# A Perceiver layer in fp32: attention chains per tile of 128 tokens instead of per half, small V weights, 64-row score products, swapped K columns

## The chip, the cores and the metric

One core of one Trainium2 chip. The metric is device time in microseconds (us) of one execution; the profile comes from one profiled execution of the same program.

## The reference, cut to what matters

Three layers run one after the other on 8 batches of 64 tokens (512 tokens) of 256 numbers, with a context of 8 batches of 1601 rows.

```python
x = x + xattn(layernorm(x), ctx)      # scores without a softmax: (Q K^T) V = Q (K^T V), then wo, residual, layer norm
x = x + attn(layernorm(x))            # causal over 64 tokens, 16 heads of 16, softmax
x = x + ffn(layernorm(x))             # attention with rotary q and k (k and v through a rank of 64), softmax, rms norm,
                                      # then a gated shared MLP and 8 experts W2 weighted by the top 2, rms norm
```

The rotary step of the third layer is `stack([x1*cos - x2*sin, x1*sin + x2*cos])` over neighbouring pairs of a head's 16 numbers. The attention of a batch is `softmax(q k^T / 4) v` for each of 16 heads.

## The kernel before, in words

The 512 tokens are four tiles of 128 tokens (two batches each). The kernel calls two tiles a half. Everything is in SBUF; there are eight PSUM banks.

*Context.* For each of the 8 batches the context (1601 x 256) is loaded in three chunks, each split into a rounded high part (ScalarE, step `split`, L514) and a low part (VectorE, L1051), and TensorE forms the Gram matrix of the batch (`gram`, banks 0 and 1, `gram_tile`). From the Gram matrix come, in the steps `evac`, `cross1` to `cross4`, the products with the key and value weights (banks 6 and 7); with the fourth batch of a half, `cross2_product` also multiplies the column sums by the value weights (`scol`).

*Chains.* For each half there is a chain: `xo_product` and `xo` (output projection and layer norm of the cross attention), `norm1`, `turn_z` (transpose), `proj1` (q, k, v of 256 tokens at a time), then for each tile `score_product` (L787: four matmuls of 128 rows by 256 columns; the keys stand in `kblk`, where the 32 rows of each pair of heads fill only their own quarter of the columns), `score` (VectorE: causal bias, maximum, subtraction; ScalarE: exponential, L550), `turn_p` (eight transposes, copied to `probT`), `sums` (sum and reciprocal), `values` (L809: eight matmuls with `probT` as the weights of 128 columns and `vblk` as 64 moving columns), the division by the sums into `on` (L1149), `turn_o` (four transposes and two VectorE operations into `aT`, L1159 and L1160) and `project` (output projection). Then `norm2`, `turn_z`, `proj2` (q; the shared rank of k and v in `kvcT`; k and v from the lower and upper 64 rows of it; q and k each multiplied by a rotation matrix `rot`, VectorE combining with sine and cosine), the same attention steps again, `rms1` and `turn_x`. The chains use PSUM banks 2 to 5, all four by `proj1` and `proj2`, and two each by the tiles.

*Dense part.* For a half: 16 `hidden_product`s in all are 8 per half (12 matmuls of 256 columns each), two `shared_product`s, eight `experts_product`s (12 matmuls of 512 columns), in banks 0, 1, 6, 7; ScalarE applies Silu (L611), VectorE multiplies, ScalarE and GpSimd split the result. Experts are summed into `Z` on VectorE (L1229), `finish` scales and adds (rstd by a power on GpSimd, L408), SP stores each tile.

*Order.* All engines walk one list of steps in the same order (`steps_in_order`: opening, first half, second half, closing); each engine runs its share of every step, in order, with semaphore waits between the engines. So a step that waits holds back whatever stands behind it on its engine. In the opening list 16 of 24 Gram chunks are done before the first half's chain; that chain lies between the other eight; the second half's chain lies between the dense steps of the first half; the closing list is the dense part of the second half. In the closing list `finish` of tiles 0, 1 and 2 stand between expert steps, and only `finish` 3 stands behind the last.

An fp32 matmul shows in the trace as two records, a transpose and a matmul on the split (fp32r) parts as one.

## Time and profile before

| what | value |
|---|---|
| median of 3 runs | 270.0 us (269.54 to 271.69) |
| the profiled execution's own time | 269.51 us |
| its span, first to last instruction | 267.7 us |
| mean granted TensorE clock | 0.992 of full |
| TensorE matmul busy | 243.5 us, 91% |
| VectorE busy | 177.8 us, 66% |
| ScalarE busy | 119.2 us, 45% |
| GpSimd busy | 69.4 us, 26% |

The time of an execution is that between its begin and end; the span lies inside it and is 1.8 us shorter here. A row of the trace names engine, line, operation, result and operands, shapes, count, then busy time. Matmuls overlap each other in the pipeline, so the distance from the start of one group to the start of the next, divided by the records between, tells what a record costs a busy TensorE; the durations shown are longer.

### The profile page before, as it was taken

The page shows a single profiled execution, that of the slowest core. Times are in us where ns is not written, and L with a number is a line of the kernel's source. Part 1 is how long each engine was busy: PE and PEld are TensorE (multiplying, and loading weights), DVE is VectorE, ACT ScalarE, POOL GpSimd, SP SyncE. Part 2 cuts the span into 40 slices and gives each one's busy share as a digit, 9 for nine tenths or more (in the row PEclk, how much of TensorE's full clock was granted, in tenths as well). Part 3 has the DMA queues.
Part 4 walks back from the last instruction along what each step waited for, and adds up shares of the span by engine and source line. Part 5 has one row for each costly group of instructions (what it writes and reads, how often), then busy time and mean ns, then how long its engine had stood idle before and what let it go on. Part 6 is the DMA issues. An engine that isn't in the chain of part 4 may idle for free.

```text
span 267.7 us, 4160 instructions
## 1 busy us (share of the span) xinstructions
PE 243.5 (91%) x1562; PEld 217.0 (81%) x1562; DVE 177.8 (66%) x376; ACT 119.2 (45%) x205; POOL 69.4 (26%) x74
## 2 busy tenths in 40 slices
PE   1988989999989999988977999999889989999991
PEld 2978989998979999777966998787658968998880
DVE  2545882696984997477767486997378556348463
ACT  4525745435175372273714599761363214541000
POOL 4011120212123023011661343797400010340010
PEclk9999999999999999999997999999999999999999
DMA  6999768775534020200020002252000000000010
GB/s 200 394 396 402 232 176 307 240 254 157 169 90 155 2 73 5 82 0 0 4 78 0 2 0 80 81 142 94 0 2 0 0 0 2 0 2 0 21 39 20
DMA packets 8851, 26.11 MB, mean 98 GB/s; under 512 B 1400, under 2 KB 3200, under 8 KB 8576
## 3 DMA queue, kind: packets, MB, share of 16 engines
q1 hardware_dynamic: 8832, 25.86, 28.6%
q8 instruction: 12, 0.20, 0.3%
q14 instruction: 7, 0.06, 0.1%
HBM read 25.33 MB, written 0.52 MB: 97 GB/s over the span
## 4 chain that ended last, share of the span: by engine, by line
PE 74%; DVE 8%; ACT 7%; issue 6%; DMA 2%; SPq 1%; POOL 1%; POOLq 0%; DVEq 0%; ACTq 0%
PE ps L627 68%; PE ps L630 6%; DMA raw<-in_ctx 2%; DVE prob L1137 1%; SPq L353 1%; POOL rstd L408 1%; DVE mx L1136 1%; DVE Z L950 1%; ACT prob L550 1%; DVE on L1149 1%; ACT raw L478 1%; ACT L611 1%; ACT kblk L542 1%; DVE kblk L1191 1%; ACT L598 0%
## 5 line engine op out<-in xcount | busy, mean ns | idle before, releaser
L627 PE MATMUL ps<-ch 128*128 128x130 f32 (+1 forms) x208 | 53.6, 274 | 5.5 <-ACT ch L507 5.4
L627 PE MATMUL ps<-ch,cl 128*128 128x260 f32 (+1 forms) x208 | 53.3, 317 | 0.0
L627 PE MATMUL ps<-w,hT 128*128 128x512 f32 x192 | 47.3, 401 | 0.0
L627 PEld LDWEIGHTS ps<-ch 128*128 128x128 f32 (+1 forms) x208 | 41.2, 198 | 6.3 <-ACT ch L507 5.3
L627 PEld LDWEIGHTS ps<-w,hT 128*128 128x128 f32 x192 | 35.7, 188 | 8.9 <-issue 0.5
L627 PEld LDWEIGHTS ps<-ch,cl 128*128 128x128 f32 (+1 forms) x208 | 41.0, 197 | 0.4 <-issue 0.2
L1051 DVE TENSOR_TENSOR cl<-raw,ch 128x1024 fp32r<-128x1024 f32 (+1 forms) x31 | 30.8, 1025 | 7.5 <-ACT ch L514 7.3
L514 ACT ACTIVATE ch<-raw 128x1024 fp32r<-128x1024 f32 (+1 forms) x31 | 26.3, 887 | 14.2 <-DMA raw<-in_ctx 8.3
L408 POOL TENSOR_TENSOR rstd<-ve,half_exp 128x2 f32<-128x2 f32 (+1 forms) x14 | 9.5, 678 | 78.3 <-DVE ve L922 78.2
L627 PE MATMUL ps<-xHL,dense 128*128 128x256 f32 x192 | 25.8, 295 | 1.5 <-DVE xHL L1200 1.5
L627 PEld LDWEIGHTS ps<-xHL,dense 128*128 128x128 f32 x192 | 24.8, 200 | 2.0 <-DVE xHL L1200 1.8
L442 POOL TENSOR_TENSOR w<-raw,w 128x1024 fp32r<-128x1024 f32 x8 | 18.9, 2370 | 16.3 <-ACT w L457 16.2
L1229 DVE SCALAR_TENSOR_TENSOR Z<-ps,w,Z 128x256 f32<-128x256 f32 x32 | 15.5, 484 | 6.7 <-PE ps L627 5.8
L425 POOL TENSOR_TENSOR gpre<-gab 128x130 f32<-128x130 f32 x16 | 7.3, 478 | 40.5 <-ACT gab L457 40.5
L442 POOL TENSOR_TENSOR dense<-stage,dense 128x1024 fp32r<-128x1024 f32 x4 | 9.5, 2384 | 29.3 <-ACT dense L457 29.3
L446 POOL TENSOR_TENSOR hT<-sa,hT 128x256 fp32r<-128x256 f32 x16 | 12.5, 795 | 16.7 <-ACT hT L457 16.7
L627 PE MATMUL ps<-kblk,qp 128*128 128x256 f32 x64 | 15.2, 383 | 0.9 <-ACT kblk L542 0.6
L550 ACT ACTIVATE prob<-prob 128x1024 f32<-128x1024 f32 x8 | 8.5, 1059 | 15.2 <-DVE prob L1137 15.1
L478 ACT ACTIVATE raw<-Z 128x256 f32<-128x256 f32 x8 | 3.3, 414 | 26.6 <-DVE Z L1229 19.4
L627 PE MATMUL ps<-w,gs 128*128 128x256 f32 x64 | 15.1, 379 | 0.0
L627 PE MATMUL ps<-vblk,probT 128*128 128x64 f32 x128 | 14.7, 273 | 0.0
L627 PEld LDWEIGHTS ps<-vblk,probT 128*128 128x128 f32 x128 | 14.6, 192 | 0.0
(162 smaller groups left out, 422.7 us busy)
## 6 DMA issues: line engine op xcount, KB each, us to landing
raw<-in_ctx SPq DMA_DIRECT2D x23, 512.0 KB, 4.3
raw<-in_w SPq DMA_DIRECT2D x8, 512.0 KB, 3.6
w<-in_w SPq DMA_DIRECT2D x2, 1024.0 KB, 9.8
stage<-in_dense SPq DMA_DIRECT2D x4, 512.0 KB, 5.8
mask<-in_mask SPq DMA_DIRECT2D x1, 800.5 KB, 9.2
rows<-in_rows SPq DMA_DIRECT2D x1, 768.0 KB, 7.9
raw<-in_ctx SPq DMA_DIRECT2D x8, 65.0 KB
raw<-in_ctx SPq DMA_DIRECT2D x4, 128.0 KB, 2.5
```

The source lines that it names most:

```text
L353: sp.dma_start(raw[:, ROWS * c + lo:ROWS * c + hi, :], src[:, c * ROWS + lo:c * ROWS + hi, :]).then_inc(sem(f"raw{c}" if n else f"first{lo ...
L408: pool.tensor_tensor(rstd[:, lo:hi], ve[:, lo:hi], half_exp[:, lo:hi], ALU.pow).then_inc(sem("rstd"), 1)
L425: last = pool.tensor_tensor(gpre[:, i % 2, k, :], gab[:, i % 2, k, k, :], gab[:, i % 2, k, k + 1, :], ALU.add)
L442: pool.tensor_tensor(piece(i, 1), raw_piece(i), f32(piece(i, 0)), ALU.subtract).then_inc(sem("piece_low"), 1)
L446: pool.tensor_tensor(hT[:, m // 4, 1, m % 4, :], sa[:, m % 4, :], f32(hT[:, m // 4, 0, m % 4, :]), ALU.subtract).then_inc(sem("h_low"), 1)
L478: act.activation(sq, Z[:, t, :], ACT.Square, scale=D ** -0.5, accum_out=ms[:, t:t + 1]).then_inc(sem("ms"), 1)
L514: last = act.activation(halves(ch[0:p, c, lo:hi, :])[:, :, :, 0:P], halves(raw[0:p, ROWS * c + lo:ROWS * c + hi, :]), ACT.Copy)
L550: act.activation(prob[:, i % 2, :, :], prob[:, i % 2, :, :], ACT.Exp, scale=SCALE).then_inc(sem("prob"), 1)
L627: return pe.matmul(o, l, r, start=start, stop=stop, skip_group_check=not check)
L630: return pe.transpose(o, src, ident)
L1051: last = dve.tensor_tensor(halves(cl[0:p, c, lo:hi, :]), halves(raw[0:p, ROWS * c + lo:ROWS * c + hi, :]), halves(f32(ch[0:p, c, lo:hi, :] ...
L1229: ins = dve.scalar_tensor_tensor(out=Z[:, t, :], in0=ps[:, DENSE_B[use % 4], e * D:(e + 1) * D], scalar=w8[:, t, 2 * u + e:2 * u + e + 1], ...
```

## The change

Every chain step is now for one tile: `xo`, `norm1`, `turn_z`, `proj1_product`, `proj2_product` and so on take a tile (four tiles instead of two halves), and even tiles use banks 4 and 5, odd tiles banks 2 and 3, with semaphores of their own (`own(name, t)` is one for even and one for odd tiles). The order of all four lists is written anew: the first tile's chain starts after two batches of context instead of four, and the two normalisations, roots and squares are cut into a part that starts the work and a part that uses the root (`norm1` and `norm1_end`, `xo` and `xo_end`, `last_square` and `last_root` and `finish`). The sums of the columns (`scol`) are multiplied every second batch. In the closing list all four `finish` steps stand behind the last expert step:

```python
("experts_product", (3, 3)), ("last_square", 2), ("experts", (3, 1)), ("experts", (3, 2)),
("experts", (3, 3)), ("last_root", 0), ("last_root", 1), ("last_square", 3), ("last_root", 2),
("last_root", 3), ("finish", 0), ("finish", 1), ("finish", 2), ("finish", 3),
```

It begins with `hidden_product` 8 right behind `turn_x` 2 and 3 (`experts_product` (1, 3) is ahead of both), and `gate_groups` 1 (an exponential) stands between `hidden_product` 9 and 10 (Silu).

Scores: eight matmuls per tile in place of four, each of 64 rows (half of the dimensions, `g`) by 128 columns, the two halves of rows into two banks:

```diff
-                    for j in range(KC):
-                        for bb in range(2):
-                            jb = j * BH + 2 * (i % 2) + bb
-                            last = mm(ps[:, tile_bank(i) + j, :].rearrange("p (r b k) -> p r b k", b=2, k=S)[:, :, bb, :],
-                                      qp[:, jb, :, :].rearrange("p h q -> p (h q)"), kblk[:, jb, :, :], True, True)
+                    for j in range(KC):
+                        for bb in range(2):
+                            for g in range(2):
+                                dims = slice(g * P // 2, (g + 1) * P // 2)
+                                got = ps[:, tile_bank(t) + g, :].rearrange("p (j r b k) -> p j r b k", j=KC, b=2, k=S)
+                                last = mm(got[:, j, :, bb, :], qp[dims, t % 2, 2 * j + bb, :, :].rearrange("p h q -> p (h q)"),
+                                          kblk[dims, t % 2, 2 * j + bb, :, :], True, True)
```

`kblk` is filled by two ScalarE copies scaled with a 0/1 column (`side32`) instead of four copies of 32 rows; no zeros are needed in it.

Values: the V block is now the weights (64 keys by 32 columns, `vz`) and `probT` moves (64 columns), 32 matmuls per tile in place of eight, and the result comes out transposed, on 32 partitions each:

```diff
-                    for c in range(H // 2):
-                        last = mm(ps[:, tile_bank(i), c * 4 * HD:(c + 1) * 4 * HD], probT[:, i % 2, c, :],
-                                  vblk[:, i % 2, c, :, :].rearrange("p b d -> p (b d)"), True, True)
+                    spots = [(r, bb) for r in range(4) for bb in range(2)]
+                    for j in range(KC):
+                        for hl in range(2):
+                            for r, bb in spots:
+                                keys = slice(bb * S, bb * S + S)
+                                last = mm(ps[32 * r:32 * r + 32, tile_bank(t) + bb, j * S:(j + 1) * S], vz[keys, t % 2, 4 * j + r, hl, :],
+                                          probT[keys, t % 2, 4 * (r // 2) + 2 * j + r % 2, hl * S:(hl + 1) * S], hl == 0, hl == 1)
```

So `turn_o`, `on` and the two VectorE operations behind it are gone; one ScalarE copy makes `aT`. The division by the sums is now made on the 1024 probabilities of a row, ahead of `turn_p` (step `shares`):

```diff
-                    link(dve.tensor_reduce(sm[:, k, :], prob[:, k, :, :].rearrange("p c (b k) -> p (c b) k", b=2), AX.X, ALU.add))
+                    link(dve.tensor_reduce(sm[:, k, :], rows_of, AX.X, ALU.add))
                     link(dve.reciprocal(rs[:, k, :], sm[:, k, :]))
+                    dve.tensor_tensor(rows_of, rows_of, rs[:, k, :].unsqueeze(2).to_broadcast([P, H, S]),
+                                      ALU.mult).then_inc(own("shares", t), 1)
```

Rotary k: the weights `wkv` hold the k columns twice, once with neighbours swapped, so k and swapped k come from four matmuls of 64 rows by 128 columns (`keys2`), and the product of k with `rot` and its copy `ks` are gone. The sign is in the sine. q is still multiplied by `rot` (256 columns per tile).

```diff
-                    mm(ps[:, CHAIN_B, :], const("rot"), ks[:, :, :].rearrange("p c n -> p (c n)"),
-                       True, True).then_inc(sem("rot"), 1)
+                    for swapped in range(2):
+                        for ob in range(KC):
+                            last = mm(ps[:, tile_bank(i), swapped * D + ob * P:swapped * D + (ob + 1) * P],
+                                      wkv[0:P // 2, swapped, ob * P:(ob + 1) * P], kvcT[i % 2][0:P // 2, :], True, True)
```

## Rows read from the trace of the kernel before

**Rows 1.** The page: busy time, and the granted clock in 40 slices.

```profile
PE 243.5 (91%) x1562; PEld 217.0 (81%) x1562; DVE 177.8 (66%) x376; ACT 119.2 (45%) x205; POOL 69.4 (26%) x74
PEclk9999999999999999999997999999999999999999
```

**Rows 2.** The page: the chain that ended last, share of the span.

```profile
PE 74%; DVE 8%; ACT 7%; issue 6%; DMA 2%; SPq 1%; POOL 1%; POOLq 0%; DVEq 0%; ACTq 0%
```

**Rows 3.** The waits of PE: us in total, times, longest.

```profile
PE ps L630 <- ACT prob L550: 1.6, 2, 1.1
PE ps L627 <- DVE xHL L1200: 1.5, 1, 1.5
PE ps L627 <- ACT ks L457: 1.3, 2, 0.7
PE ps L627 <- DVE ctxT L1100: 1.2, 1, 1.2
```

**Rows 4.** Windows: busy times of PE, PEld, DVE, ACT, POOL, then PEclk.

```profile
143.30:159.80 16.50, 16.48 (x109) 15.89 (x109) 11.58 (x41) 11.50 (x21) 5.44 (x6) 0.90 0.00 1
```

**Rows 5.** Timeline of PE, one score product: start, us, group.

```profile
119.79 1.95 PE L627 MATMUL ps<-kblk,qp 128*128 128x256 f32 x8
121.57 0.55 PE L627 MATMUL ps<-q0T,mb 128*128 128x64 f32 x4
```

**Rows 6.** Timeline of PE, values of two tiles and what follows.

```profile
96.12 3.68 PE L627 MATMUL ps<-vblk,probT 128*128 128x64 f32 x32
99.64 1.11 PE L627 MATMUL ps<-cv,w 128*128 128x128 f32 x8
```

**Rows 7.** Timeline of PE in the first proj2: products of 64 rows.

```profile
112.71 1.11 PE L627 MATMUL ps<-qs,cst 128*128 128x512 f32 x2
113.76 0.48 PE L627 MATMUL ps<-kvcT,wkv 64*128 64x256 f32 x1
113.77 0.48 PE L627 MATMUL ps<-wkv,kvcT 64*128 64x256 f32 x1
114.08 0.38 PE L627 MATMUL ps<-kvcT,wkv 64*128 64x256 f32 x1
114.52 0.38 PE L627 MATMUL ps<-wkv,kvcT 64*128 64x256 f32 x1
```

**Rows 8.** Timeline of PE, narrow windows: first record, then the ones behind it.

```profile
85.67 0.22 PE L627 MATMUL ps<-q0T,mb 128*128 128x64 f32 x1
85.72 0.39 PE L627 MATMUL ps<-q0T,mb 128*128 128x64 f32 x2
152.03 0.17 PE L627 MATMUL ps<-gate,xT 128*128 128x10 f32 x1
152.06 0.37 PE L627 MATMUL ps<-gate,xT 128*128 128x10 f32 x2
```

**Rows 9.** Timeline of PE: the column sums by the value weights.

```profile
128.06 0.95 PE L627 MATMUL ps<-scol,w 128*128 128x4 f32 x8
128.87 1.07 PE L630 MATMUL ps<-cst,prob 128*128 128x128 f32 x8
```

**Rows 10.** Groups by form, PE, ACT and DVE: busy us, mean ns, idle before.

```profile
L630 PE MATMUL ps<-cst,on 128*128 128x128 f32 x32 | 4.9, 280 | 0.9 <-DVE on L1149 0.9
L611 ACT ACT_TABLE_LOAD x4 | 5.1, 1283 | 0.1
L1149 DVE TENSOR_TENSOR on<-ps,rs 128x512 f32<-128x512 f32 x8 | 5.5, 692 | 4.1 <-PE ps L627 4.1
L1137 DVE TENSOR_TENSOR prob<-prob,mx 128x1024 f32<-128x1024 f32 x4 | 5.2, 1305 | 0.1
```

**Rows 11.** Timeline of the end: last products, last experts and finish.

```profile
239.49 22.55 PE L627 MATMUL ps<-w,hT 128*128 128x512 f32 x96
...
262.14 1.00 DVE L1229 SCALAR_TENSOR_TENSOR Z<-ps,w,Z 128x256 f32<-128x256 f32 x2 [1.79 <-PE ps L627]
265.12 0.42 DVE L1238 TENSOR_TENSOR X<-X,Z 128x256 f32<-128x256 f32 x1
```

More of the change, by code:

```diff
@@ L132, in second_half_steps @@
-        ("piece", 8), ("turn_p", 5), ("sums", 5), ("shared", 0), ("shared", 1), ("experts", (0, 0)), ("values", 4),
-        ("values", 5), ("piece", 9), ("turn_o", 4), ("turn_o", 5), ("piece", 10), ("project", 4), ("project", 5),
-        ("experts_product", (0, 1)), ("experts_product", (0, 2)), ("piece", 11), ("norm2", 1), ("experts", (0, 1)),
-        ("turn_z", (1, 1)), ("piece", 12), ("experts", (0, 2)), ("proj2", 1), ("experts_product", (0, 3)),
-        ("score_product", 6), ("experts", (0, 3)), ("score", 6), ("score_product", 7), ("experts_product", (1, 0)),
@@ L137, in second_half_steps @@
-        ("turn_p", 6), ("score", 7), ("experts_product", (1, 1)), ("sums", 6), ("turn_p", 7), ("sums", 7),
-        ("experts", (1, 0)), ("values", 6), ("values", 7), ("turn_o", 6), ("turn_o", 7), ("project", 6),
-        ("project", 7), ("experts_product", (1, 2)), ("rms1", 1), ("experts", (1, 1)), ("experts", (1, 2)),
-        ("turn_x", 1), ("experts_product", (1, 3)),
+        ("norm1", 1), ("split", 16), ("proj2_product", 0), ("rotate", 0), ("evac", 4), ("keys2", 0), ("values2", 0),
+        ("roped", 0), ("gram", 15), ("keys_roped", 0), ("norm1_end", 1), ("cross1", 4), ("turn_z", (1, 0)),
@@ L867, in _ @@
                     if m == 0:
-                        pe.wait_ge(sem("xL"), i // 8 + 1)
+                        for t in range(TH):
+                            pe.wait_ge(own("xL", t), i // 8 + 1)
                         pe.wait_ge(sem("piece_low"), 4)
```

777 lines of the change are left out of this document (386 added, 391 removed), and 3 rows, old and new, of the table USES.

## The prediction

> **What bounds the kernel now.** I read the page first. TensorE (PE) is busy 91% of the span, VectorE 66%, ScalarE 45% [rows 1], and the chain that ended last runs 74% through PE [rows 2]. So what counts is PE's own time plus the gaps in which it waits, and the change has to be priced in two sums: records on PE, and gaps. The waits of PE [rows 3] are short and many; apart from the first load they come from the chains of the halves: 1.6 us for the exponentials, 1.5 for the low part of x, 1.3 for the copy of k before its rotation, 1.2 for the cross attention of the second half, and 0.9 for the division by the sums [rows 10]. One gap costs twice: behind the wait for x the granted clock falls; over the 16.5 us from 143.3 it is 0.90 [rows 4], which is 3.3 us at the lower of the two levels (1.2 GHz instead of 2.4), and costs half of that, some 1.6 us. At the end nothing overlaps: the last products stop at 239.49 + 22.55 = 262.04, and the last addition ends at 265.54 [rows 11].
>
> **The change part by part.** All sums are against the profiled execution, 269.5 us with a span of 267.7; it lies 0.5 below the median of 270.0, and I treat that as noise.
>
> *Scores.* A tile's score product is 8 records that hold PE for 121.57 - 119.79 = 1.78 us, 0.22 each; its row says 1.95, so 0.17 of a row's time is the pipeline's end [rows 5]. With 128 columns a record costs half: eight of them show 1.07 us, less 0.17, over 8, is 0.11 [rows 9]. After, there are 16 records in two row groups. Whether two groups run side by side the trace does show: in `proj2` the product of k on the lower 64 rows and that of v on the upper 64 start 0.01 us apart, though the four records of one stand wholly behind the four of the other in the program, and the eight records, 1.76 us in a row, are through in 114.52 - 113.76 + 0.22 = 0.98 us [rows 7]. So 16 x 0.11 / 2 = 0.88, a saving of 0.85 per score product, 8 of them: -6.8 us. The bound on the other side is no overlap: 1.76, saving nothing.
>
> *Turning the result.* 32 transposes [rows 10] of 0.11 go: -3.5.
>
> *Values.* Now 16 records per tile at 3.52 / 32 = 0.11, 1.76 us per tile [rows 6]; these are held by the loading of 128 weight columns, for 64 moving columns alone take 85.72 - 85.67 = 0.05 to 0.056 us [rows 8]. After, 64 records per tile, each with 32 weight columns and 64 moving ones, on eight places of the array (two row groups, four column groups). No row shows such a record. From above, with no overlap at all: 0.056 each, 3.6 us per tile, +14.6 us over 8 tiles and kinds (64 x 0.056 = 3.58; less 1.76; times 8). From below, if column groups overlap as well as row groups: 0.014 each, 0.9 per tile, -6.9 us. In between, two row groups overlapping give 0.028, which is also the shortest distance between two matmuls that the trace has: 152.06 - 152.03 [rows 8]. I take 0.028: 1.79 per tile, +0.2 us.
>
> *Entering the 64-row products.* The second record of the q rotation begins 0.52 after the first and streams 0.43, so PE would be free at 113.66; the first 64-row record then takes 0.32 where the next takes 0.22 [rows 7]. Entering the other form costs 113.76 - 113.66 + 0.10 = 0.2 us. The kernel entered it twice and now does so some 20 times (8 scores, 8 values, 4 `keys2`): +3.6. What leaving costs no row shows; between 0 and the same again. I take 4.0. The Trainium skill has this as a rule, in "TensorEngine Tiling (Array Packing)", Key Properties: a change of tiling mode drains the array first. The row agrees with it, with 0.2 us; it is the rule that speaks against splitting the products, for the gain of the scores alone (0.85) has to pay two such changes each time.
>
> *Sums and rotation.* `scol` by the value weights is 8 records of 0.81 us [rows 9], made four times instead of two: +1.6. Rotary k: the rotation was two records of at least 0.43 per half with the wait for `ks` [rows 3, 7], the k and v products 1.1 per half. After, per tile: k and swapped k 8 records of 0.11 = 0.88, with v beside them in the other rows, and 0.43 for q as before. Per half 2 x 0.9 + 0.2 against 0.86 + 1.1: +0.4 in all.
>
> *Gaps that go.* The wait for `on` 0.9, for `ks` 1.3, most of that for the exponentials, the cross attention, the low part of x and the slow clock behind it (1.6 + 1.2 + 1.5 + 1.6) because four chains of half the size interleave with the Gram chunks and the experts: at best -8, of which I count -7.5.
>
> *Gaps that come.* Each `proj2` waits behind its `turn_z` for the copy, now four times, and `keys2` for `kvcT`; the two waits for which halves paid (0.7 for a copy at a time, rows 3) become some +2 to +3. The division is now ahead of `turn_p`, on 1024 values: 1.3 us for the like operation, against 0.69 for `on` [rows 10], so from score to `turn_p` 1.3 us more must be covered 8 times by other products; behind it the chain is shorter by as much (no `on`, no `turn_o`). I take +1 for that. Behind `values` stands a ScalarE copy instead; in one place, tile 0's second kind, no product stands between: +0.6. Together +4.
>
> *The closing list.* `turn_x` 2 and 3 now stand right ahead of `hidden_product` 8: two rounds of copy, low part and copy in turn, where the one round of a half was a wait of 1.5 [rows 3] behind a single product; I count one tile's round more: +1.3. Between Silu of `hidden_product` 9 and 10 there is an exponential: two more table loads of 1.28 us on ScalarE [rows 10], against three banks of products that are ahead of it: +0.5. And the end: `finish` 0 to 2, hidden between products now, come behind the last expert. Before, 3.5 us lay between last product and last addition [rows 11]; after, VectorE has three more pairs of 0.48 + 0.42 (2.7), of which GpSimd's power of the last tile (0.55) hides a little: +2.2, sure to lie on the path. Nothing is gained for it, for PE had no gap among the last 96 products.
>
> *Sum.* -6.8 - 3.5 + 0.2 + 4.0 + 1.6 + 0.4 - 7.5 + 4 + 1.3 + 0.5 + 2.2 = -3.6. 269.5 - 3.6 = 265.9: I predict 266 us.
>
> **The rivals.**
>
> *Small matmuls don't overlap (slower).* PE runs the 512 value records one after the other at 0.056 us or more. For it: 128 instructions (weights and matmul) must be issued per tile where 32 were, and the shortest distance in the trace, 0.028, is that of single pairs, never of a row of 64; the mean over any long run is 0.06 us per instruction or slower. Against it: the two groups of [rows 7]. It costs 14.6 - 0.2 = 14.4: 280 us. The change turns slower once a value record costs over 0.028 + 3.6/512 = 0.035 us. On a page: "TensorE: Matmul & The Clock Gate" of the Trainium skill, Part 1, gives some 62 ns per matmul where the sequencer's firmware decodes them, and 25 ns where hardware does; by the first it would be an estimated 3 us more still. No row here tells which holds.
>
> *The column groups overlap too (faster).* Records at 0.014 us: 6.9 + 0.2 below my sum, 259 us. For it: nothing in the code orders the eight places; against it: no row has ever two column groups.
>
> *The chain of a tile is too long (slower).* Score, exponential, sum, division, transposes, copies lie in series; where no Gram chunk or expert covers them, 1.3 us of division per tile and kind and the late copies show, 8 x (1.3 + 0.3) = 12.8 less the 1.6 counted for them above, so +11: 277. Against it: VectorE's work hardly changes, and every list has dense products between the chain's steps.
>
> *The gain is given back (same).* The gaps only move: without the -7.5 but with half of it, 269.7.
>
> **How the numbers follow.** My case has 0.38, the fast rival 0.20, the slow matmuls 0.22, the long chain 0.10, given back 0.10. The range of 8 in 10 reaches from 256 (the fast rival with a little more) to 280 (the slow one); my own case alone is 262 to 270. Within 1% of 270.0, 2.7 us, is about what a measurement of this kernel can't tell from no change. Faster by more than 1% (below 267.3) are the fast rival and nearly three quarters of my case: 0.48. Same: a quarter of my case and the given-back one: 0.20. Slower: 0.32.
>
> **What would show each step right or wrong.** A score product of 16 records in about 0.9 to 1.1 us, in pairs 0.01 apart; values of 64 records in 1.8 us (0.9: fast rival; 3.6: slow one); no `turn_o`; waits of PE summing to no more than before, without `ks` and `on`; the clock at its upper level all through the middle; and 5.7 us instead of 3.5 between the last product and the last addition. I am wrong if the values take over 2.3 us per tile, or if the waits of PE grow.

## The result, and the profile after

The changed kernel takes 272.35 us (median of 5 runs, 270.98 to 273.15) against 269.9 us before (5 runs, 268.52 to 271.69): a ratio of 1.0105, 95% interval 1.0054 to 1.0157. It is slower by one per cent where I forecast 266 us: inside my range of 256 to 280, but on the other side of the kernel before. The ratios leave out executions more than 1.5% above the fastest of their kernel: three of the seven of `a_tail` and one of the ten of `a_clock8`. The profiled execution took 273.15 us with a span of 271.2, before 269.51 and 267.7; the working below is on the spans, +3.5.

The page of the kernel after: busy time, granted clock in 40 slices, and the chain that ended last. They answer to [rows 1, 2].

```profile
PE 238.5 (88%) x2074; PEld 211.1 (78%) x2074; DVE 180.0 (66%) x386; ACT 123.5 (46%) x241; POOL 76.3 (28%) x85
PEclk9999999999999999999997997999999995999998
...
PE 64%; DVE 15%; ACT 9%; DMA 4%; issue 4%; POOL 2%; SPq 1%; POOLq 0%; DVEq 0%
```

TensorE's busy time fell, from 243.5 to 238.5 us. But 88% of a longer span leaves 32.7 us idle where 24.2 were, and the chain that ended last runs 64% through TensorE where it was 74%; VectorE's share in it went from 8% to 15%. Before any line is looked at, this says that the saving was made and turned into waiting.

Where it happened shows a table by stage. The cuts are the first record of `hidden_product` 0, the first of `hidden_product` 8 and the end of the last product. The windows view of the kernel before (window, length, then busy time and count of PE, PEld, DVE, ACT, POOL, then clock, DMA share and GB/s):

```profile
0.00:143.30 143.30, 129.25 (x894) 118.98 (x894) 97.96 (x185) 66.38 (x110) 31.98 (x41) 1.00 0.47 160
143.30:224.40 81.10, 76.60 (x444) 65.15 (x445) 58.41 (x124) 42.08 (x68) 29.48 (x21) 0.98 0.11 33
224.40:262.04 37.64, 37.64 (x225) 32.89 (x223) 19.42 (x63) 10.19 (x27) 7.39 (x11) 1.00 0.03 11
262.04:267.70 5.66, 0.00 (x0) 0.00 (x0) 2.03 (x5) 0.51 (x2) 0.54 (x1) 0.92 0.07 23
```

The same view of the kernel after:

```profile
0.00:147.20 147.20, 128.53 (x1166) 115.92 (x1167) 103.61 (x200) 70.14 (x130) 38.76 (x49) 0.99 0.47 160
147.20:222.82 75.62, 69.12 (x687) 59.12 (x685) 55.57 (x120) 40.12 (x81) 29.52 (x24) 0.96 0.10 29
222.82:263.64 40.82, 40.82 (x224) 36.07 (x224) 16.02 (x52) 12.69 (x29) 5.70 (x8) 0.92 0.00 1
263.64:271.20 7.56, 0.00 (x0) 0.00 (x0) 4.77 (x14) 0.51 (x2) 2.33 (x4) 0.83 0.21 69
```

Length less PE's busy time is PE's idle time. Read so, the four stages are:

- up to `hidden_product` 0: +3.9 us, of which idle 14.05 to 18.67 (+4.6) and busy -0.7;
- to `hidden_product` 8: -5.5 us, idle 4.5 to 6.5 (+2.0), busy -7.5;
- to the last product: +3.2 us, no idle time in either; the same products at a mean clock of 0.92 instead of 1.00;
- behind it: +1.9 us.

So the middle did gain, and three other stages took more than that back. The first figure scatters. In six profiled executions with this opening (the kernel after, `a_again`, `a_clock8`, `a_tail`, `a_tail_clock`, `a_double`) the idle time up to `hidden_product` 0 is 16.3 to 18.8 us; with the opening of the kernel before it is 14.1, and 16.2 in `b_scores`. Of the +4.6, some 2 us can be chance.

**The products.** The timeline of PE of the kernel after, one score product, then values of one tile and of two:

```profile
126.62 1.16 PE L653 MATMUL ps<-kblk,qp 64*128 64x128 f32 x16 [0.36 <-ACT kblk L493]
127.72 0.48 PE L653 MATMUL ps<-w,gs 128*128 128x256 f32 x1
...
136.09 0.86 PE L653 MATMUL ps<-probT,vz 64*32 64x64 f32 x64 [0.34 <-ACT probT L481]
136.88 0.66 PE L656 MATMUL ps<-cst,gab 128*128 128x128 f32 x4
...
213.79 1.67 PE L653 MATMUL ps<-probT,vz 64*32 64x64 f32 x128
215.39 0.91 PE L653 MATMUL ps<-wo,aT 128*128 128x256 f32 x3
```

A score product holds PE for 127.72 - 126.62 = 1.10 us where it was 1.78 [rows 5]. The values of a tile hold it for 136.88 - 136.09 = 0.79, and 128 records in a row take 215.39 - 213.79 = 1.60: 0.0125 us per record, a little less than even the fast rival's 0.014.

To see what each kind of product is worth over the whole span, I added, record by record, the time by which its end lies beyond the latest end before it; these sum to the busy times of the page. The groups that changed, before and after, in us:

```
values                    14.08   6.61   -7.5
scores                    14.54   9.35   -5.2
turning the result         4.30   0      -4.3
k rotated                  2.25   0      -2.3
k and v from the rank      2.15   5.04   +2.9   (k twice, in 64-row form)
q rotated                  1.90   2.26   +0.4
column sums by wv          1.58   3.14   +1.6
hidden and gates          26.16  28.83   +2.7   (nearly all lower clock)
all others               176.52 183.24   +6.7
```

The lower clock is in these sums. In the profile before, TensorE worked at the lower level for 3.4 us in the middle of the kernel, behind the first `turn_x`; after, it did so for 13.4 us, in three stretches that begin at 145.7, 166.2 and 224.2 us and last 3.4, 3.4 and 6.8. Each such microsecond costs half of itself, so the clock costs 6.7 us instead of 1.7: +5.0 us. Of these 2.4 lie in the hidden and gate products, 0.7 in the scores and 2.0 in the last line, where `w,ctxT` +1.0 and the transposes of the probabilities +0.8 are the clock and hardly anything else. What is left of the last line, +4.7, is spread thinly: `w,gs` +1.0, `cv,w` +0.8, `zT,wq` +0.6 and so on, each with the same work as before. I take these for records behind a wait or a 64-row group; no run takes them apart. Other executions show the same clocks: the five of the kernel after have a mean of 0.968 to 0.983, and those of the kernel before that were timed beside the experiments 0.993 to 0.999, mostly 0.997 or more, where the profiled one had 0.992. So most executions of the kernel before have no such stretch in the middle at all.

Put together on the two profiles: products at the upper clock -10.0, the clock +5.0, idle time up to `hidden_product` 8 +6.6, the end +1.9, which is the +3.5 of the span.

**The waits.** The waits of PE after (us in total, times, longest), to be held against [rows 3]:

```profile
PE ps L653 <- ACT ch L530: 5.7, 1, 5.7
PE ps L653 <- issue: 2.8, 3, 1.9
PE ps L653 <- DVE qp L1149: 1.8, 2, 1.3
PE ps L653 <- ACT probT L481: 1.8, 3, 0.7
PE ps L653 <- DVE cl L1072: 1.5, 1, 1.5
PE ps L653 <- DVE ctxT L1121: 1.4, 2, 1.1
...
PE ps L653 <- ACT aT L481: 1.0, 1, 1.0
...
PE ps L653 <- ACT vz L487: 1.0, 1, 1.0
PE ps L653 <- ACT zT L481: 0.9, 2, 0.5
...
PE ps L656 <- DVE prob L1172: 0.8, 2, 0.4
```

`ks` and `on` are gone, as said. The wait for `ctxT` is still there, and that for x (`xHL`) has become the 1.9 us that the view calls issue, ahead of `hidden_product` 8. New are the queries `qp`, the turned probabilities `probT`, the copy `vz` and the low part of the context `cl`; the waits for `aT` and `zT` were 0.5 and 0.7 us before and are 1.0 and 0.9. Over all rows of this view the sum went from 18.3 to 24.2 us.

The wait for `cl` can't be put down to the new order. It is 1.9 us in `b_scores`, which has the order of the kernel before, and 0.2 or 0.3 us in `a_tail_clock` and `a_tail`, which have the new opening. Among kernels with the new opening it is longest where TensorE reaches its upper clock early (at 9.2 us in the kernel after, at 14.8 in those two), `c_fill` apart.

### The profile page after: what moved, and what is told of

The parts are those of the page before. It is cut to its first block, busy times and chain, and to the rows that moved or that the text cites. A ratio compares the mean times of both kernels' runs of the same rounds, so it can differ in the third digit from the quotient of the medians.

```text
span 271.2 us, 5245 instructions
## 1 busy us (share of the span) xinstructions
PE 238.5 (88%) x2074; PEld 211.1 (78%) x2074; DVE 180.0 (66%) x386; ACT 123.5 (46%) x241; POOL 76.3 (28%) x85
## 4 chain that ended last, share of the span: by engine, by line
PE 64%; DVE 15%; ACT 9%; DMA 4%; issue 4%; POOL 2%; SPq 1%; POOLq 0%; DVEq 0%
PE ps L653 60%; PE ps L656 4%; DMA X<-in_x 3%; POOL rstd L433 2%; ACT ch L537 2%; ACT probT L481 2%; DMA raw<-in_ctx 2%; DVE Z L975 2%; DVE prob L1163 1%; DVE mx L1162 1%; ACT prob L574 1%; DVE st L952 1%; DVE cl L1072 1%; DVE prob L1172 1%; DVE prob L1160 1%
## 5 line engine op out<-in xcount | busy, mean ns | idle before, releaser
L433 POOL TENSOR_TENSOR rstd<-ve,half_exp 128x1 f32<-128x1 f32 (+1 forms) x22 | 15.3, 700 | 114.3 <-DVE ve L947 114.3
L653 PE MATMUL ps<-xHL,dense 128*128 128x256 f32 x192 | 28.0, 308 | 1.9 <-issue 1.9
L653 PEld LDWEIGHTS ps<-xHL,dense 128*128 128x128 f32 x192 | 26.5, 213 | 2.6 <-issue 2.1
L468 POOL TENSOR_TENSOR w<-raw,w 128x1024 fp32r<-128x1024 f32 x8 | 20.3, 2548 | 9.6 <-ACT w L481 9.6
L481 ACT ACTIVATE probT<-ps 128x512 f32<-128x512 f32 x16 | 8.8, 596 | 18.5 <-PE ps L656 18.5
L500 ACT ACTIVATE sq<-Z 128x256 f32<-128x256 f32 x8 | 3.3, 414 | 26.6 <-DVE Z L1237 21.9
L653 PEld LDWEIGHTS ps<-w,gs 128*128 128x128 f32 x64 | 11.6, 190 | 2.8 <-DVE gs L1085 1.2
L1225 DVE TENSOR_TENSOR sa<-sa,ps 128x256 f32<-128x256 f32 x16 | 6.4, 418 | 9.4 <-ACT sa L637 9.3
L637 ACT ACTIVATE sa<-ps 128x256 f32<-128x256 f32 x16 | 6.1, 383 | 13.3 <-PE ps L653 13.1
L1170 DVE TENSOR_REDUCE sm<-prob 128x16 f32<-128x1024 f32 x8 | 9.7, 1218 | 2.1 <-ACT prob L574 2.0
```

The source lines that it names most:

```text
L433: pool.tensor_tensor(rstd[:, lo:hi], ve[:, lo:hi], half_exp[:, lo:hi], ALU.pow).then_inc(sem("rstd"), 1)
L468: pool.tensor_tensor(piece(i, 1), raw_piece(i), f32(piece(i, 0)), ALU.subtract).then_inc(sem("piece_low"), 1)
L481: act.activation(dst, src, ACT.Copy).then_inc(signal, 1)
L653: return pe.matmul(o, l, r, start=start, stop=stop, skip_group_check=not check)
L1170: link(dve.tensor_reduce(sm[:, k, :], rows_of, AX.X, ALU.add))
L1225: dve.tensor_tensor(sa[:, m % 4, :], sa[:, m % 4, :], ps[:, DENSE_B[use % 4], TOK:2 * TOK], ALU.mult).then_inc(sem("taken"), 1)
```

## The experiments

Each kernel was timed beside the kernel before on the same chip, and all ratios are to the kernel before. The new kernel unchanged, on another chip, as a measure of the scatter:

> The changed kernel itself, unchanged, on the chip of this call, so that the repairs and the single parts are compared beside it. Expected 1.0105 of before again; if it comes out at 1.00 or 1.02, the distances found so far between variants are no better known than that.

Measured: 272.14 us, 1.0112 (1.0049 to 1.0175).

### The closing list: the ends and the clock

The lower clock in the last long stage begins right behind the gap ahead of `hidden_product` 8. `a_clock8` puts products there whose result nobody reads:

```diff
+                    if i == 8:
+                        for k in range(8):
+                            mm(ps[:, CHAIN_B + 3, :], hT[:, 1, 0, k % 4, 0:P], w2[:, 3, 0, k % 4, :], True, True)
                     if m == 0:
                         for t in range(TH):
                             pe.wait_ge(own("xL", t), i // 8 + 1)
```

> The changed kernel, with eight matmuls of 512 columns (some 1.9 us, their result never read) in the gap of 2 us ahead of hidden_product 8. Theory: the gap itself costs 2 us, and the lower clock that follows it (6.8 us at the lower level, 224.2 to 231.1) costs 3.4 us more; with PE kept busy the clock stays at its upper level and the kernel gets about 3.4 us faster by doing more work. Rival: the clock falls for another reason (the small value products before), or the extra products come on top: no gain, or 1 to 2 us slower.

Measured: 270.07 us, 1.0045 (1.0004 to 1.0086). Its windows view of the last products:

```profile
222.40:260.10 37.70, 37.69 (x224) 32.95 (x224) 16.02 (x52) 12.59 (x29) 5.70 (x8) 1.00 0.00 1
```

Its timeline of PE around `hidden_product` 8, and below it that of the kernel after:

```profile
220.21 2.11 PE L653 MATMUL ps<-w,hT 128*128 128x512 f32 x8
222.38 1.67 PE L653 MATMUL ps<-xHL,dense 128*128 128x256 f32 x12
```

```profile
220.02 0.87 PE L656 MATMUL ps<-cst,Z 128*128 128x128 f32 x4
222.82 1.76 PE L653 MATMUL ps<-xHL,dense 128*128 128x256 f32 x12 [1.93 <-issue]
```

The eight products fill the 1.93 us in which PE did nothing, `hidden_product` 8 starts as late as ever, and the stage behind it takes 37.7 us instead of 40.8, with the clock at 1.00 instead of 0.92. The gap itself is what the copies of `turn_x` take; the 3.1 us are the clock that falls behind it, 6.8 us long at the lower level, and these were in no term of my sum. The profiled executions differ by 1.3% (273.15 and 269.60), the ratios by 0.6%, which is 1.6 us and half of the 3.4 that I expected, and their intervals overlap; what is shown best is the stage.

That filling the gap keeps the clock up is shown; that the gap alone brings it down is not. `a_double`, further below, has the same gap and a closing stage at the upper level:

```profile
226.88 1.67 PE L653 MATMUL ps<-xHL,dense 128*128 128x256 f32 x12 [1.93 <-issue]
226.88:264.59 37.71, 37.71 (x224) 32.97 (x224) 16.02 (x52) 12.59 (x29) 5.69 (x8) 1.00 0.00 1
```

Of the five profiled executions that leave the gap open, three (the kernel after, `a_again`, `a_tail`) have 6.8 us at the lower level behind it, `a_open` has 3.4 and `a_double` none. Of the seven that fill it none has any.

`a_tail` puts the roots and `finish` 0 to 2 back between the expert steps:

```diff
...
-        ("experts", (3, 3)), ("last_root", 0), ("last_root", 1), ("last_square", 3), ("last_root", 2),
-        ("last_root", 3), ("finish", 0), ("finish", 1), ("finish", 2), ("finish", 3),
+        ("last_root", 0), ("last_root", 1), ("experts", (2, 0)), ("finish", 0), ("experts", (2, 1)),
+        ("finish", 1), ("experts_product", (3, 0)), ("experts_product", (3, 1)),
...
+        ("last_root", 2), ("experts_product", (3, 3)), ("experts", (3, 1)), ("finish", 2), ("experts", (3, 2)),
+        ("experts", (3, 3)), ("last_square", 3), ("last_root", 3), ("finish", 3),
```

> The changed kernel, with finish 0, 1 and 2 and their roots put back between the expert steps of the closing list. If the end is lost time of its own (theory: the three finishes behind the last product cost 2.0 us, 5.5 against 3.5 us from last product to last addition), the span shrinks by 2.0 us and nothing else moves. Rival: VectorE, loaded again between the experts, holds back the products, and the gain is under 0.5 us.

Measured: 268.67 us (the median of all seven executions), 0.9947 (0.9907 to 0.9986). Last product to end of span took 5.6 us instead of 7.6. The timeline of the end in the kernel after shows what was taken off it, one pair of 0.48 and 0.42 us per tile (of VectorE only):

```profile
265.60 0.48 DVE L975 SCALAR_TENSOR_TENSOR Z<-Z,rstd,rows 128x256 f32<-128x256 f32 x1
266.12 0.42 DVE L1246 TENSOR_TENSOR X<-X,Z 128x256 f32<-128x256 f32 x1
...
268.18 0.48 DVE L975 SCALAR_TENSOR_TENSOR Z<-Z,rstd,rows 128x256 f32<-128x256 f32 x1
268.69 0.42 DVE L1246 TENSOR_TENSOR X<-X,Z 128x256 f32<-128x256 f32 x1
```

The ratios differ by 1.6% or 4 us, more than the 2 us that this explains. Taken over all seven executions the mean is 1.001 of the kernel before, 2.6 us under the new kernel. The 2 us of the end are shown by the profile; the rest is not shown to be an effect of the edit.

Both together (`a_tail_clock`):

> The changed kernel with both repairs: finish 0 to 2 back between the expert steps, and eight unused matmuls in the gap ahead of hidden_product 8. If the two losses are separate, 2.0 and up to 3.4 us add up and it runs 4 to 5.5 us under the changed kernel, 1 to 2.5 us under the one before; if they are one and the same, it is no better than the better of the two (0.995 of before).

Measured: 267.08 us, 0.9921 (0.9864 to 0.9978). With the two repairs the new kernel is faster than the one before, by 0.8%. That accounts for what the closing list cost; what is left is why 7 us less work of TensorE's own (238.0 us busy against 243.5, of which the unused products are nearly 2) give only 2 us.

### The opening

`a_open` moves the first normalisation behind `split` 4, so that the low part of the context isn't late (the wait for `cl` of 1.5 us), and swaps two products:

```diff
-        ("split", 0), ("gram", 0), ("split", 1), ("split", 2), ("split", 3), ("norm0", 0), ("gram", 1), ("gram", 2),
-        ("evac", 0), ("split", 4), ("norm0_end", 0), ("cross1", 0), ("split", 5), ("gram", 3), ("gram", 4),
-        ("pre", 0), ("cross2_product", 0), ("qb", 0), ("flag", 0), ("norm0", 1), ("gram", 5), ("cross2", 0),
+        ("split", 0), ("gram", 0), ("split", 1), ("split", 2), ("split", 3), ("gram", 1), ("gram", 2),
+        ("evac", 0), ("split", 4), ("norm0", 0), ("cross1", 0), ("norm0_end", 0), ("split", 5), ("gram", 3), ("gram", 4),
+        ("cross2_product", 0), ("pre", 0), ("gram", 5), ("qb", 0), ("flag", 0), ("norm0", 1), ("cross2", 0),
```

> The changed kernel, with norm0 of the first half behind split 4 on VectorE, so that the wait for x no longer holds back the low part of a context chunk, and a Gram chunk put between pre 0 and qb 0. Theory: the gap of 1.6 us at 17.8 closes to 0.3 and the kernel is 1 to 1.5 us faster. Rival: the opening is bound by the loads anyway, or the late normalisation opens a gap of the same size before pre 0: no gain.

Measured: 274.75 us, 1.0196 (1.0149 to 1.0243): slower where I expected it to be faster. The waits of PE in it:

```profile
PE ps L653 <- ACT z0T L481: 3.2, 2, 2.4
PE ps L653 <- issue: 2.9, 3, 1.9
PE ps L653 <- ACT probT L481: 1.8, 3, 0.7
PE ps L653 <- DVE qp L1149: 1.5, 2, 1.3
PE ps L653 <- DVE ctxT L1121: 1.4, 2, 1.1
PE ps L653 <- DVE gs L1085: 1.4, 1, 1.4
```

The wait for `cl` is 1.0 us instead of 1.5, and the copy of `z0T`, now behind two splits on ScalarE, is late by 2.4 us, `gs` by 1.4. Behind the wait for `z0T` the clock is at the lower level for another 3.4 us, from 35.8 on. The last Gram product starts at 137.5 us instead of 131.8. Not all of that is the edit: in this execution the upper clock came at 15.3 us instead of 9.2, so that the Gram products took 2.0 us more. And since the wait for `cl` varies from 0.2 to 2.0 us without the edit, it was not what to aim at.

### What a microsecond of TensorE is worth in the new order

`a_double` makes the values twice (`for j in (0, 1, 0, 1)` in place of `for j in range(KC)`), 512 more records:

> The changed kernel, with every value product made twice: 512 records more. At 0.0125 us a record that is 0.8 us per tile and kind, 6.4 us in all. If PE bounds the stretches in which the values lie, the kernel is 5 to 7 us slower; if they lie in gaps that the chain of a tile leaves, so that the time saved on them turned into waiting, it is under 3 us slower.

Measured: 274.68 us, 1.0196 (1.0126 to 1.0265), 0.9% or 2.4 us above the new kernel, for work of 512 x 0.0125 = 6.4 us. In the profile `hidden_product` 0 starts at 148.9 instead of 147.2, 1.7 us later for 3.2 us of work, and `hidden_product` 8 at 226.9 instead of 222.8, 4.1 us later for 6.4. The last stage then lacks the lower clock, which gives some of it back. So about two thirds of the added work shows, as far as one execution of each can tell. By the bounds that I had set, the 2.4 us speak for values that lie in gaps (under 3 us), but the clock of the last stage alone (3.1 us) makes up the difference to those that don't (5 us or more).

`c_wide` puts the size of the old score product back into `a_tail_clock`, 8 records of 128 rows and 256 columns. The columns are those of two key blocks, so the true scores are left out; the work of the other engines stays.

```diff
-                            for g in range(2):
-                                dims = slice(g * P // 2, (g + 1) * P // 2)
...
+                            got = ps[:, tile_bank(t) + j, :].rearrange("p (r b k) -> p r b k", b=2, k=S)
+                            last = mm(got[:, :, bb, :], qp[:, t % 2, 2 * j + bb, :, :].rearrange("p h q -> p (h q)"),
+                                      kblk[:, t % 2, 2 * j:2 * j + 2, :, :].rearrange("p b g k -> p (b g) k"), True, True)
```

> The changed kernel with its last additions spread and with unused products ahead of hidden_product 8 (a_tail_clock, 0.9921), with each score product put back to 8 records of 128 rows and 256 columns (the columns are those of two blocks of keys, so the scores are not those of the layer; same work for the engines otherwise). Theory 1, TensorE's own time sets the pace in the new order too: the 16 records took 1.10 us per product and the 8 take 1.78, 8 times, so +5.4 us, a ratio of 1.012. Theory 2, in the new order waits of the tile chains set a good part of the pace, as half of the doubled value work stayed hidden: +2 to +3 us, a ratio of 1.000 to 1.003. In the old order the same product change was worth 3.8 to 4 us.

Measured: 271.46 us, 1.0097 (1.0056 to 1.0138), 1.8% or 4.7 us above `a_tail_clock` for 5.4 us of work. In the profile `hidden_product` 0 starts at 149.4 instead of 146.5, 2.9 us later for 2.7 us of work. Theory 1 is much the nearer one: the new order isn't so slack that TensorE's time no longer counts. Of what is added, between two thirds (`a_double`) and nearly all (`c_wide`) shows. So what was saved in the products was worth most of its size in the new order as well, and the loss should lie in what the order itself adds. That is a conclusion from what is left over: no kernel here has the new order with all of the old products.

### One part alone on the kernel before

`b_values` gives the kernel before only the small V weights. That form multiplies the probabilities by the reciprocals ahead of the transposes, so `turn_p` has to wait for the sums where it waited only for the exponential:

```diff
                 elif step == "turn_p":
-                    pe.wait_ge(sem("prob"), i + 1)
+                    pe.wait_ge(sem("shares"), i + 1)
```

> The kernel before, its order and its chains per half kept, with one part of the change: the small V weights, thus the division ahead of the transposes, no transposes of the result and a ScalarE copy into aT. The changed kernel showed a value product of 64 records in 0.8 us (1.76 before), so PE has 8 x 0.96 + 3.5 = 11 us less to do. Theory (the parts are good, the new order and the chains per tile lost it): 3 to 8 us faster than before. Rival (the longer way from scores to transposes opens as many gaps as the short products close, in any order): within 1 us of before, or slower.

Measured: 304.77 us, 1.131 (1.1239 to 1.1381). Its waits of PE:

```profile
PE ps L634 <- DVE prob L1145: 31.9, 8, 5.8
PE ps L631 <- ACT ch L507: 5.5, 1, 5.5
PE ps L631 <- DVE ctxT L1100: 2.9, 1, 2.9
PE ps L631 <- DVE xHL L1185: 1.5, 1, 1.5
```

Eight waits, one per tile and kind, 4 us each. PE's waits sum to 52.1 us instead of 18.3, +33.8. The clock adds: its mean is 0.921, with seven stretches of 6.8 us at the lower level. TensorE works for 34.6 us of them, which costs 17.3 us where it was 1.7. Against both stand products that are 13.7 us cheaper at the upper clock; together that is the +35.6 us of span. With the row groups of the scores as well (`b_both`):

> As b_values, with the scores in row groups of 64 too (16 records of 128 columns in 1.1 us in place of 1.78, so 5.4 us less on PE; kblk filled by two ScalarE copies of 512 columns instead of four copies of 32 rows). Theory: 5 to 12 us faster than before, 2 to 5 beyond b_values. Rival: the chain, not PE, ends last at the scores, and this adds nothing (under 1 us) to b_values.

Measured: 301.83 us, 1.1212 (1.1139 to 1.1284). The scores add some 3 us of gain, as the theory had it, to a kernel that is far slower than either case assumed. Was it only that the list of the kernel before has `sums` behind `turn_p`, so that on VectorE something stands ahead of the division? `b_order` exchanges the two in every tile:

> b_both with sums and turn_p exchanged in the list, so that the sum and the division of a tile stand ahead of the next tile's scores on VectorE, and PE comes to the transposes one dense step later. In b_values and b_both PE waited 32 us for the division. Theory (head of line: the 33 us came from the order, PE standing before transposes whose input VectorE makes only after the next tile's scores): most of it goes, 15 us or more faster than b_both. Rival (the chain itself is too long for two tiles at a time): under 8 us faster than b_both.

Measured: 294.06 us, 1.0896 (1.085 to 1.0942). The waits of PE:

```profile
PE ps L636 <- DVE prob L1148: 28.2, 5, 9.2
PE ps L633 <- ACT ch L510: 5.2, 1, 5.2
PE ps L633 <- DVE ctxT L1103: 2.9, 1, 2.9
```

8 us better than `b_both`, and the wait, 32.8 us there, is still 28.2. The order of these two steps is not the main cause. What is left as the explanation is that the chain from the scores to the transposes is too long for the products that the old list has between them; only this one exchange was tried.

`b_scores` gives the kernel before only the scores in row groups (`kblk` filled by two scaled copies, the rotated keys added up in one VectorE operation instead of three, the reciprocals stored in the new order of heads):

```diff
                         for bb in range(2):
                             jb = j * BH + 2 * (i % 2) + bb
-                            last = mm(ps[:, tile_bank(i) + j, :].rearrange("p (r b k) -> p r b k", b=2, k=S)[:, :, bb, :],
-                                      qp[:, jb, :, :].rearrange("p h q -> p (h q)"), kblk[:, jb, :, :], True, True)
+                            for half in range(2):
+                                dims = slice(half * P // 2, (half + 1) * P // 2)
+                                got = ps[:, tile_bank(i) + half, :].rearrange("p (j r b k) -> p j r b k", j=KC, b=2, k=S)
+                                last = mm(got[:, j, :, bb, :], qp[dims, jb, :, :].rearrange("p h q -> p (h q)"),
+                                          kblk[dims, jb, :, :], True, True)
```

> The kernel before with the scores in row groups alone; values, division and transposes of the result stay, and the order of the steps is untouched. No operation is added to the way from scores to result, and PE has some 5 us less to do. Theory (a part that shortens PE without lengthening the chain pays even in the old order): 2 to 5 us faster than before. Rival (in the old order the chain of a half, not PE, sets the end, so any PE time saved turns into waiting): within 1 us.

Measured: 265.49 us, 0.9858 (0.9805 to 0.991), the fastest of all kernels here. Its page:

```profile
PE 238.0 (90%) x1626; PEld 211.9 (80%) x1626; DVE 175.5 (66%) x372; ACT 117.1 (44%) x201; POOL 68.1 (26%) x73
```

PE's busy time is 238.0 us, as low as that of the whole change (238.5): -5.5 us, with the idle time up by only 264.1 - 238.0 - 24.2 = 1.9. So everything else in the change (cheaper values, no turning, swapped columns, a chain per tile) took nothing off PE's busy time on balance, the lower clock that it brought included (5.0 us), and added 6.6 us of idle time (32.7 against 26.1).

### Is it the division, and can a wait be closed?

`a_nodiv` is `a_tail_clock` without the multiplication of the probabilities (the division is left out of the computation; a copy of one column stands in its place):

> The kernel with two repairs, with the division of the probabilities left out (the sums are still formed and signalled, so the result lacks the division by them). 8 x 1.3 us less on VectorE and on the way from scores to transposes. If the chains of the tiles set the end in the middle of the kernel, it is 3 us or more faster than with the division; if the lists cover it, under 1.5 us.

Measured: 266.05 us, 0.9886 (0.9849 to 0.9923), a difference to 0.9921 that its interval doesn't tell from none. In the new order the 1.3 us of division are covered, or nearly.

`a_best` tried to close two gaps of `a_tail_clock`: three unused products ahead of the last `xo_product`, and the queries of tile 2 ahead of `gate_experts` on VectorE, because PE waits for `qp` twice there, 1.8 us in all.

> The changed kernel with the two repairs, and with three unused matmuls in the wait ahead of the last xo_product and the queries of tile 2 ahead of the expert gates on VectorE. If the lower clock after hidden_product 0 comes from that wait, 1.7 us more go, and with the 0.5 us of the queries it is 1 to 2 us under the kernel with two repairs (0.985 of before). Rival: the clock falls anyway, or VectorE comes later elsewhere: no difference.

Measured: 273.86 us, 1.0143 (1.0087 to 1.02), slower where I expected it to be faster. Its two edits apart:

```diff
+                    if i == T - 1:
+                        for k in range(3):
+                            mm(ps[:, CHAIN_B + 3, 0:D], ident, w0[:, 3, 0, :], True, True)
                     pe.wait_ge(sem("corrected"), i + 1)
```

> a_tail_clock with only the three unused products ahead of the last xo_product, one of the two edits of a_best. If they are what made a_best slow (they ran at the lower clock and held back xo_product 3): about +4 to +6 us over a_tail_clock, ratio 1.008 to 1.014. If the order of queries and gate_experts is to blame, this one stays within 1 us of a_tail_clock, 0.989 to 0.996.

```diff
-        ("turn_z", (2, 0)), ("proj1_product", 2), ("gate_experts", 0), ("queries", 2), ("keys1", 2), ("gate_best", 0),
+        ("turn_z", (2, 0)), ("proj1_product", 2), ("queries", 2), ("keys1", 2), ("gate_experts", 0),
...
-        ("score", (2, 0)), ("piece", 7), ("proj1_product", 3), ("queries", 3), ("exp", (2, 0)), ("keys1", 3),
+        ("score", (2, 0)), ("piece", 7), ("proj1_product", 3), ("queries", 3), ("gate_best", 0), ("exp", (2, 0)), ("keys1", 3),
```

> a_tail_clock with only the queries of tile 2 moved ahead of gate_experts, and gate_best behind the queries of tile 3, the other edit of a_best. If the chain on VectorE and ScalarE is what holds the tiles (the wait for vz of 4.0 us): PE's wait for qp of 1.3 us goes, a longer one for vz comes, +4 to +6 us over a_tail_clock, ratio 1.008 to 1.014. If not: the wait for qp goes and nothing comes, 0.986 to 0.992.

Measured: the products alone 267.34 us, 0.992 (0.9878 to 0.9962), no change, though in the profiled execution the clock now stays at the upper level from 14.3 us to the last product; the order alone 272.52 us, 1.0127 (1.0092 to 1.0163), all of the loss. The waits of PE with the order changed:

```profile
PE ps L653 <- ACT vz L487: 4.0, 1, 4.0
```

and the timelines that tell how it comes about, of ScalarE:

```profile
165.28 0.82 ACT L493 ACTIVATE kblk<-ps,cst 128x256 f32<-128x256 f32 x2
168.96 0.42 ACT L481 ACTIVATE hT<-sa 128x256 fp32r<-128x256 f32 x1 [2.85 <-DVE sa L1228]
169.28 0.42 ACT L487 ACTIVATE vz<-ps 128x128 f32<-128x128 f32 x2
```

and of VectorE:

```profile
163.72 0.87 DVE L1152 TENSOR_SCALAR qp<-ps,cst 128x256 f32<-128x256 f32 x2
164.50 0.16 DVE L1017 TENSOR_REDUCE esum<-pe 128x2 f32<-128x16 f32 x1
...
168.07 0.17 DVE L1034 TENSOR_TENSOR w<-w,w8a 128x16 f32<-128x16 f32 x1
168.50 0.42 DVE L1228 TENSOR_TENSOR sa<-sa,ps 128x256 f32<-128x256 f32 x1 [0.25 <-DVE w L1034]
```

`gate_best`, a row of small operations from 164.50 to 168.24, now stands ahead of VectorE's part of `hidden` 0 (168.50). ScalarE's copy `hT` waits 2.85 us for that, and the copy `vz` for tile 3 stands behind it in ScalarE's queue: 169.28 instead of 164.29 in `a_tail_clock`. PE's score product of tile 3 waits for `vz`. The waits for `qp` fell only from 1.8 to 1.2 us, that for `vz` grew from 1.0 to 4.0, and there is a lower clock for 6.8 us twice where `a_tail_clock` had it once for 3.4. A tile's chain passes three engines, and on each it stands in one queue with work of the dense part.

## Why the prediction was wrong

The step that failed is that of the gaps: those that go, *"at best -8, of which I count -7.5"*, against *"Together +4"* for those that come. I counted -3.5 for both. Of the -7.5, some 1.6 were clock, so on idle time alone, the closing start and the table loads included, I had about nothing; PE's idle time rose by 6.6 us up to `hidden_product` 8. The second half of the same step is the clock: I had it at -1.6 us (*"and the slow clock behind it"*), and it cost 5.0 us more than before. Each of the two alone turns the sign. My own signs had it: the waits of PE were to grow if I was wrong, and the clock was to stay at its upper level all through the middle. By its points:

- **Gaps that go.** Only `ks` and `on` went (1.3 and 0.9) and half of the wait for the exponentials, now for the division behind them (1.6 to 0.8). The cross attention (1.2 to 1.4) and x (1.5 to 1.9) stayed. The lower clock behind x, which I counted as won, is not there in most executions of the kernel before, so there was little to win; the new order has three such stretches. I had argued that four half-size chains interleave better; but a chain of half the size has as many steps in series, each with its copies, and there are twice as many of them. That this is why the waits grew fits the rows, but no run shows it apart.
- **Gaps that come.** I counted two sorts, copies ahead of `proj2` and the division. The division isn't seen (`a_nodiv`). Seen are `qp` 1.8, `probT` 1.8, `vz` 1.0 and somewhat longer waits for `aT` and `zT`: late operations on VectorE and ScalarE. I had looked for these nowhere, and VectorE's +2 and ScalarE's +4 us of busy time gave no sign of them. The first stage is where idle time rose most, but 1.5 us of its +4.6 are the wait for `cl`, which comes and goes in either order.
- **Values**, +0.2: mis-sized; they measured -7.5. I had taken 0.028 us as the shortest distance between two matmuls of the trace, while my own [rows 7] have them 0.01 us apart. The fast rival's reason holds, row and column groups run side by side. The Trainium skill, "TensorE: Matmul & The Clock Gate", Part 1, says that matmuls never start less than about 25 ns apart. Here 64 matmuls of the program, shown as 128 records, took 1.60 us, which is 25 ns for one of the program and 12.5 ns for a record on average. As a mean over matmuls of the program the rule agrees; as a bound on single starts it doesn't, for the records of one tile start as little as 6 ns apart. The 62 ns of the firmware path, by which I made the slow rival slower, is not seen.
- **Scores**, -6.8, and entering the 64-row form, +4.0: scores measured -5.2, in that 1.10 us includes the entering (16 x 0.11 / 2 = 0.88, and 0.2), so 1.6 of the 4.0 is in there. The rest of the entering is not seen by itself; it can only lie in the +4.7 of the other groups. Also in the measured -5.2 are 0.7 us of lower clock. The form is worth its price: `b_scores` is 4 us faster. The rule of the Trainium skill that I had weighed against the split ("TensorEngine Tiling (Array Packing)", Key Properties: a change of mode drains the array) agrees, at this 0.2 us.
- **Turning**, -3.5: -4.3. **Sums**, +1.6: +1.6. **Rotary k**, +0.4 (my own terms give only +0.1): k, v and q together -2.3 + 2.9 + 0.4 = +1.0.
- **Closing start**, +1.3, and **table loads**, +0.5: the table loads show nothing, the stage takes 37.7 us in `a_clock8` as before. The gap is 1.9 us, and behind it the clock is down for 6.8 us: 3.1 us of a kind that I had seen in the profile before, behind the other `turn_x` [rows 4], and had priced only as going away.
- **End**, +2.2: +1.9.

All of PE's records together I had at -6.8 - 3.5 + 0.2 + 4.0 + 1.6 + 0.4 = -4.1, and the busy time fell by 5.0. That is near by luck: values were 7.7 cheaper than priced, and 5.0 us came back as slower clock and 4.7 as the thin surcharge on other records. Of the rivals, the fast one was right in its mechanism and wrong in the time, since other losses eat its gain. "The chain of a tile is too long" came nearest, but the division, its mechanism, is covered in the new order (`a_nodiv`); that it is the number of hand-overs instead is my reading of the waits. On the old list it is the main part: 1.131.

What the change does, then: the small V weights need a longer chain ahead of the transposes. Without the new order that costs 35 us. The new order hides most of it, but adds waits, a lower clock and an uncovered end, together more than the cheaper values and the row groups give. Shown by runs are that filling the gap keeps the closing clock up, the end, the worth of the score product (in both orders) and the waits for the division on the old list. That the new order was needed is shown for this old list and one exchange in it, not for every list. Not shown is what each wait and each of the two earlier stretches of lower clock cost, nor the chains per tile and the swapped K columns, which no run has alone; the two attempts on the waits (`a_open`, `a_best`) ended slower.

## What to carry to other kernels

When a change makes products cheaper and also moves steps, price the order by the steps of its chains: for each step the queue that it stands in on every engine, and what stands ahead of it there; a mean busy share of 66% on an engine says nothing about it. Test each part alone on the old kernel, for one part may carry all of the gain (`b_scores`, 0.9858) and another may force the rest (`b_values`, 1.131). A gap of 2 us ahead of a long dense stretch is worth filling with products that nobody reads where the trace shows the clock falling behind it (3.1 us here; `a_double` had the gap without the fall). Read the clock of several executions before it is priced, and of their starts before a small wait there is explained. And no final scaling should stand behind the last product that could stand ahead of it.

## What the runs showed of the hardware that was not expected

Values records of 64 rows, 32 weight columns and 64 moving columns, on eight places of the array, take 0.0125 us each in a row of 128, where 128-row records with 64 moving columns in their old form took 0.11. The gap of 1.93 us ahead of `hidden_product` 8 was followed by 6.8 us at a clock of 1.2 GHz and cost 3.1 us; with the products of `a_clock8` in that gap the clock stayed at 2.4 GHz, and so it did in `a_double` with the gap open. At the start of the profiled executions the upper level comes between 8.9 and 16.3 us after the first instruction, and at 9.2 or 14.8 us with one and the same opening; up to there the full Gram products of 260 columns are 0.22 us apart, then 0.12. How much of a run lies at the lower level differs between the kernels more than their waits do (3.4 us ahead of the end in `a_tail_clock`, 13.6 in the kernel after, some 48 in `b_values`), and it grows the differences that waits make.
